# Negated row maxima turned by VectorE in squares of 32 by 32, and sent in four pieces each, in a macaron transformer block

## What is computed

```python
x = x + 0.5 * ffn(layernorm(x))        # weights are signs, hidden width 2048, relu
x = x + attention(layernorm(x))        # 16 heads of 32, w_q, w_k, w_v, w_o
x = x + 0.5 * ffn(layernorm(x))

# attention, per batch and head
scores = einsum('bhqd,bhkd->bhqk', q, k) * SCALE
probs = softmax(scores, axis=-1)
attn = einsum('bhqk,bhkd->bhqd', probs, v)
```

## Time and profile before

| | |
|---|---|
| median of 3 runs | 2874.53 us (2872.97 to 2876.33) |
| the profiled execution | 2881.08 us, span 2879.0 us, mean granted clock of PE 0.997 of full speed |
| PE busy | 2846.1 us, 99% of the span |
| DVE busy | 2041.4 us, 71% |
| ACT busy | 1607.7 us, 56% |
| POOL busy | 1372.8 us, 48% |
| DMA | 424.28 MB in 184375 packets, mean 147 GB/s |
| attention | from about 790 to about 2330 us of the span |

### The profile page before, as it was taken

The page is one execution under the profiler, slowest core; times in us unless marked ns, Lnnn a source line. Parts: engine busy times, 40 slices in busy tenths (PEclk is TensorE's granted clock), DMA queues, the critical chain, the costliest instruction groups (busy, mean ns, idle before and its releaser), DMA issues.

```text
span 2879.0 us, 37964 instructions
## 1 busy us (share of the span) xinstructions
PE 2846.1 (99%) x14288; PEld 1949.0 (68%) x14288; DVE 2041.4 (71%) x3037; ACT 1607.7 (56%) x2850; POOL 1372.8 (48%) x487
## 2 busy tenths in 40 slices
PE   8999999999999999999999999999999999999999
PEld 6888888887755555555555555555555468888887
DVE  5655556768888888888888888888888446555553
ACT  6344434332276767767677777676777654333333
POOL 0000000000089999989898899898988620000000
PEclk9999999999999999999999999999999999999999
DMA  5111112555389999999999999999999962222210
GB/s 190 31 58 30 30 30 71 200 194 188 136 175 194 200 203 202 201 200 203 201 202 204 197 203 202 201 200 200 203 200 204 209 179 59 59 59 59 59 30 30
DMA packets 184375, 424.28 MB, mean 147 GB/s; under 512 B 89728, under 2 KB 90752, under 8 KB 148224
## 3 DMA queue, kind: packets, MB, share of 16 engines
q0 software_dynamic: 31824, 231.75, 39.2%
q1 hardware_dynamic: 152368, 190.11, 24.1%
HBM read 121.91 MB, written 67.63 MB: 66 GB/s over the span
## 4 chain that ended last, share of the span: by engine, by line
PE 84%; DMA 7%; POOL 3%; DVE 3%; issue 2%; ACT 1%; SPq 0%; POOLq 0%; DVEq 0%; ACTq 0%
PE bank L624 16%; PE bank L601 15%; PE bank L1064 15%; PE bank L1060 13%; PE bank L1091 13%; PE bank L743 7%; DMA att_dma_acc<-att_p 3%; PE bank L451 3%; POOL att_acc L924 3%; DMA att_dma_acc<-att_dma_acc 2%; PE bank L1118 1%; DMA prob_sums<-head_total 1%; DMA head_tot_t<-prob_sums 0%; PE bank L240 0%; DMA op_inv_second<-prob_inverse 0%
## 5 line engine op out<-in xcount | busy, mean ns | idle before, releaser
L975 DVE TENSOR_REDUCE att_row_max<-bank 128x1 f32<-128x512 f32 x2048 | 1249.3, 681 | 209.3 <-PE bank L1064 209.1
L924 POOL TENSOR_TENSOR att_acc<-att_acc,att_p 128x2048 f32<-128x2048 f32 x217 | 1079.8, 4976 | 19.7 <-ACT att_p L1044 13.0
L1044 ACT ACTIVATE att_p<-bank 128x512 f32<-128x512 f32 x1792 | 919.4, 617 | 289.3 <-PE bank L1060 286.2
L1064 PE MATMUL bank<-att_k,att_q 96*128 96x512 f32 x2048 | 834.0, 409 | 2.9 <-DVE att_row_max L975 2.6
L1060 PE MATMUL bank<-att_q,att_k 98*128 98x512 f32 x2048 | 810.3, 399 | 6.0 <-ACT att_p L1044 6.0
L1064 PEld LDWEIGHTS bank<-att_k,att_q 96*128 96x128 f32 x2048 | 387.2, 189 | 275.0 <-DVE att_row_max L975 123.2
L1060 PEld LDWEIGHTS bank<-att_q,att_k 98*128 98x128 f32 x2048 | 386.8, 189 | 116.7 <-ACT att_p L1044 17.6
L573 ACT ACTIVATE ffn_hid<-bank,up_s 128x512 f32<-128x512 f32 x256 | 176.3, 689 | 517.2 <-PE bank L601 505.7
L521 DVE TENSOR_TENSOR ffn_hid_lo<-ffn_hid,ffn_hid_hi 128x512 fp32r<-128x512 f32 x256 | 175.7, 691 | 383.7 <-ACT ffn_hid_hi L576 383.7
L1091 PE MATMUL bank<-att_p,att_v 128*32 128x512 f32 x3584 | 434.6, 601 | 0.0
L601 PE MATMUL bank<-hi,ffn_up_w 128*128 128x512 f32 x1024 | 400.7, 391 | 5.7 <-DVE lo L189 3.8
(11 more groups left out here) (116 smaller groups left out, 2378.8 us busy)
## 6 DMA issues: line engine op xcount, KB each, us to landing
att_dma_acc<-att_p POOLq DMA_DIRECT2D x161, 1024.0 KB, 10.6
att_dma_acc<-att_dma_acc POOLq DMA_DIRECT2D x30, 1024.0 KB, 11.9
att_dma_acc<-att_acc POOLq DMA_DIRECT2D x30, 1024.0 KB, 6.9
att_q<-q_hi SPq DMA_DIRECT2D x64, 256.0 KB, 4.1
att_k<-k_hi SPq DMA_DIRECT2D x64, 256.0 KB, 6.7
x<-x_after_ffn SPq DMA_DIRECT2D x15, 1024.0 KB, 7.3
x_after_ffn<-x_out SPq DMA_DIRECT2D x8, 1024.0 KB, 9.9
q_hi<-qkv_o_hi SPq DMA_DIRECT2D x32, 256.0 KB, 2.0
```

What stands on the lines that cost most here:

```text
L924: self.nc.gpsimd.tensor_tensor(self.acc[H % 2][:], a[:], self.tile(H, kt)[:], ALU.add).then_inc(self.summed, 1)
L975: self.nc.vector.tensor_reduce(self.row_max[odd][:, qt, q:q + 1], m[:], axis=AX.X, op=ALU.max).then_inc(self.m_read, 1)
L1044: self.nc.scalar.activation(into[:, q * CH:(q + 1) * CH], self.score_bank(H, kt, q)[:], ACT.Exp, scale=SCALE).then_inc(self.exp_done, 1)
L1064: self.nc.tensor.matmul(m[:], self.q_st[T % NB][0:KQ, qt * P:(qt + 1) * P], self.k_st[T % NB][0:KQ, q * CH:(q + 1) * CH], start=True, stop ...
```

## The change

The negated maxima stay with DVE. neg_max becomes 128 x 32, with columns 16 to 31 zero (set once, in the first head). DVE turns it in four squares of 32 by 32, one for each 32 partitions, into neg_t; so partition 32 i + t of neg_t holds queries 32 i to 32 i + 31 of query tile t. The cast and the subtraction work on 128 x 32 in SBUF. SP sends each of the two rows in four transfers, each from 16 partitions of 32 values, in pieces of 128 bytes. The turn's place in the ring of banks goes (65 places a head), with PE's waits for DVE around it; `rows_out` stands directly behind `negate`. The last head waits for sums_copied before its sums, since these go to bank 3 without a place in the ring that would do it. PE waits for eight transfers a head in place of two.

```diff
--- before.py
+++ after.py
@@ -759,12 +759,14 @@
 UNITS = KT * QC
 AHEAD = LEAD * QC
 GROUP_ENDS, LAST_ENDS = (9, 18, 27, 36, 45, 54, 64), tuple(range(8, 65, 8))
-SUMS_AFTER = TURN_AFTER = 4
-SUMS_AT = TURN_AT = GROUP_ENDS[SUMS_AFTER]
-SLOTS = UNITS + 2
+SUMS_AFTER = 4
+SUMS_AT = GROUP_ENDS[SUMS_AFTER]
+SLOTS = UNITS + 1
 CHAINS = 2
 PER = 7 * 16
-NEG = 3
+NEG = 4
+TURN = 32
+NEG_LOADS = 2 * 16 * (P // TURN)
 ALONE_FROM = 3
 
 
@@ -791,10 +793,10 @@
 
 def slot(p):
 
-    return p + (p >= SUMS_AT) + (p >= TURN_AT)
-
-
-TURN_SLOT, SUMS_SLOT = TURN_AT, SUMS_AT + 1
+    return p + (p >= SUMS_AT)
+
+
+SUMS_SLOT = SUMS_AT
 AT_SLOT = {slot(p): p for p in range(UNITS)}
 
 
@@ -860,13 +862,13 @@
         self.dma_acc = [[c.sb(f"att_dma_acc{i}_{x}", at, [P, SEQ]) for x, at in enumerate(ats)]
                         for i, ats in enumerate(((WORK_AT, SUM_AT), (LO1_AT, X1_AT)))]
         self.row_max = [c.sb(f"att_row_max{i}", HEAD_AT + 4 + 0.25 * i, [P, KT, QC]) for i in range(2)]
-        self.neg_max = c.sb("att_neg_max", HEAD_AT + 4.5, [P, KT])
-        self.neg_hi, self.neg_lo = c.sb("att_neg_hi", HEAD_AT + 5, [KT, P], F32R), c.sb("att_neg_lo", HEAD_AT + 5.5, [KT, P], F32R)
+        self.neg_max, self.neg_t = c.sb("att_neg_max", HEAD_AT + 4.5, [P, TURN]), c.sb("att_neg_t", HEAD_AT + 4.625, [P, TURN])
+        self.neg_hi, self.neg_lo = c.sb("att_neg_hi", HEAD_AT + 5, [P, TURN], F32R), c.sb("att_neg_lo", HEAD_AT + 5.5, [P, TURN], F32R)
         self.m_ps, self.s_ps, self.o_ps = c.bank[0:4], c.bank[4:7], c.bank[7]
         self.loaded = [c.sem(f"att_loaded{i}") for i in range(NB)]
         self.ones_set = c.sem("att_ones_set")
         self.m_ready, self.m_read = c.sem("att_m_ready"), c.sem("att_m_read")
-        self.neg_dve, self.neg_pe, self.neg_loaded = c.sem("att_neg_dve"), c.sem("att_neg_pe"), c.sem("att_neg_loaded")
+        self.neg_set, self.neg_dve, self.neg_loaded = c.sem("att_neg_set"), c.sem("att_neg_dve"), c.sem("att_neg_loaded")
         self.s_ready, self.exp_done, self.p_used = c.sem("att_s_ready"), c.sem("att_exp_done"), c.sem("att_p_used")
         self.summed, self.dma_summed = c.sem("att_summed"), [c.sem(f"att_dma_summed{x}") for x in range(CHAINS)]
         self.chains_joined, self.sum_joined = c.sem("att_chains_joined"), c.sem("att_sum_joined")
@@ -880,9 +882,6 @@
 
 
         return self.m_ps[3] if H >= NH - 2 else self.m_ps[m_bank(H + 1, SUMS_SLOT)]
-
-    def turn_bank(self, H):
-        return self.m_ps[m_bank(H, TURN_SLOT)]
 
 
 
@@ -897,9 +896,10 @@
 
     def max_rows(self, sp, H):
         for r, rows in enumerate((self.neg_hi, self.neg_lo)):
-            sp.wait_ge(self.neg_dve, NEG * H + 2 + r)
-            sp.dma_start(f32(self.q_st[H % NB][KQ + r:KQ + r + 1, :].rearrange("o (t p) -> o t p", p=P)),
-                         f32(rows[:])).then_inc(self.neg_loaded, 16)
+            sp.wait_ge(self.neg_dve, NEG * H + 3 + r)
+            row = self.q_st[H % NB][KQ + r:KQ + r + 1, :].rearrange("o (t i p) -> o i t p", i=P // TURN, p=TURN)
+            for i in range(P // TURN):
+                sp.dma_start(f32(row[:, i, :, :]), f32(rows[i * TURN:i * TURN + KT, :])).then_inc(self.neg_loaded, 16)
 
     def head_free(self, sp, H):
 
@@ -983,16 +983,22 @@
     def negate(self, dve, H):
         dve.wait_ge(self.m_read, UNITS * (H + 1))
         if H > 0:
-            dve.wait_ge(self.neg_pe, H)
-        self.nc.vector.tensor_reduce(self.neg_max[:], self.row_max[H % 2][:], axis=AX.X, op=ALU.max, negate=True).then_inc(self.neg_dve, 1)
-
-    def rows_out(self, dve, H, t_ps):
-        dve.wait_ge(self.neg_pe, H + 1)
+            dve.wait_ge(self.neg_dve, NEG * H)
+        else:
+            self.nc.vector.memset(self.neg_max[:], 0.0).then_inc(self.neg_set, 1)
+            dve.wait_ge(self.neg_set, 1)
+        self.nc.vector.tensor_reduce(self.neg_max[:, 0:KT], self.row_max[H % 2][:], axis=AX.X, op=ALU.max, negate=True).then_inc(self.neg_dve, 1)
+
+    def rows_out(self, dve, H):
+
+        dve.wait_ge(self.neg_dve, NEG * H + 1)
+        self.nc.vector.transpose(self.neg_t[:], self.neg_max[:]).then_inc(self.neg_dve, 1)
+        dve.wait_ge(self.neg_dve, NEG * H + 2)
         if H > 0:
-            dve.wait_ge(self.neg_loaded, 32 * H)
-        self.nc.vector.tensor_copy(self.neg_hi[:], t_ps[0:KT, 0:P]).then_inc(self.neg_dve, 1)
-        dve.wait_ge(self.neg_dve, NEG * H + 2)
-        self.nc.vector.tensor_tensor(self.neg_lo[:], t_ps[0:KT, 0:P], f32(self.neg_hi[:]), ALU.subtract).then_inc(self.neg_dve, 1)
+            dve.wait_ge(self.neg_loaded, NEG_LOADS * H)
+        self.nc.vector.tensor_copy(self.neg_hi[:], self.neg_t[:]).then_inc(self.neg_dve, 1)
+        dve.wait_ge(self.neg_dve, NEG * H + 3)
+        self.nc.vector.tensor_tensor(self.neg_lo[:], self.neg_t[:], f32(self.neg_hi[:]), ALU.subtract).then_inc(self.neg_dve, 1)
 
     def vector_tile(self, dve, H, kt):
         T = H + 1 + (kt + LEAD) // KT
@@ -1002,8 +1008,7 @@
                 self.reduce_block(dve, UNITS * (H + 1) + AHEAD + p, self.m_ps[m_bank(H, slot(p))], T % 2, (kt + LEAD) % KT, q)
             if kt == KT - LEAD and q == 0 and H + 1 < NH:
                 self.negate(dve, H + 1)
-            if p == TURN_AT - 1 and H + 1 < NH:
-                self.rows_out(dve, H + 1, self.turn_bank(H))
+                self.rows_out(dve, H + 1)
         if H > 1 and kt == 2:
             self.head_out.invert(dve, H - 2)
         if H == NH - 1 and kt == 12:
@@ -1074,13 +1079,7 @@
             pe.wait_ge(self.m_read, n - 3)
         elif 2 <= n < FOUR_FROM:
             pe.wait_ge(self.m_read, n - 1)
-        if n == UNITS:
-            pe.wait_ge(self.neg_dve, NEG)
         self.maxima(self.first_bank(n), T, n % UNITS // QC, n % QC)
-
-    def transpose_max(self, pe, H, t_ps):
-        pe.wait_ge(self.neg_dve, NEG * H + 1)
-        self.nc.tensor.transpose(t_ps[0:KT, 0:P], self.neg_max[:], self.ident[:]).then_inc(self.neg_pe, 1)
 
     def out_tile(self, pe, H, kt):
         pe.wait_ge(self.exp_done, UNITS * H + QC * (kt + 1))
@@ -1125,8 +1124,6 @@
             old -= MR
         if old == SUMS_SLOT:
             pe.wait_ge(self.head_out.sums_copied, H)
-        elif old == TURN_SLOT:
-            pe.wait_ge(self.neg_dve, NEG * (H + 2))
         elif old < 0:
             pe.wait_ge(self.m_read, UNITS * (H + 1) + AHEAD + old + 1)
         else:
@@ -1135,7 +1132,7 @@
     def tensor_group(self, pe, H, u, beside=None):
 
         if u == 0:
-            pe.wait_ge(self.neg_loaded, 32 * (H + 1))
+            pe.wait_ge(self.neg_loaded, NEG_LOADS * (H + 1))
             pe.wait_ge(self.ones_set, min(H + 1, NB))
         ends = group_ends(H)
         begin = ends[u - 1] if u > 0 else 0
@@ -1159,11 +1156,10 @@
         if H < NH - 1 or u < ALONE_FROM:
             for kt in range(complete(H, u - 2), complete(H, u - 1)):
                 self.out_tile(pe, H, kt)
-        if u == TURN_AFTER and H + 1 < NH:
-            self.bank_free(pe, H, TURN_SLOT)
-            self.transpose_max(pe, H + 1, self.turn_bank(H))
         if u == sums_after(H) and H > 0:
             self.bank_free(pe, H, SUMS_SLOT)
+            if H == NH - 1:
+                pe.wait_ge(self.head_out.sums_copied, H - 1)
             self.sums(pe, H - 1)
 
 
@@ -1394,8 +1390,7 @@
                             ffn1.add_input(dve, NCH - 1)
                         if (n, t) == (FIRST_TURN[0], FIRST_TURN[1] - 1):
                             att.negate(dve, 0)
-                        if (n, t) == FIRST_TURN:
-                            att.rows_out(dve, 0, att.m_ps[2])
+                            att.rows_out(dve, 0)
 
                 for H in range(NH):
                     for kt in range(KT):
@@ -1505,8 +1500,6 @@
                         qkv.tensor(pe, n, t, between)
                         for b in range(count // 2, count):
                             att.first_maxima(pe, first + b)
-                        if (n, t) == FIRST_TURN:
-                            att.transpose_max(pe, 0, att.m_ps[2])
 
                 pe.wait_ge(qkv.qk_read, 8 * NCH)
                 pe.wait_ge(qkv.v_read, 4 * NCH)
@@ -1519,7 +1512,6 @@
                             first = (H, end, i) == (LAST - 1, UNITS, 0)
                             if first:
                                 pe.wait_ge(att.m_read, UNITS * NH)
-                                pe.wait_ge(att.neg_dve, NEG * NH)
                                 pe.wait_ge(wo_done, DT + 1)
                             if (H, end) == (LAST - 1, UNITS) or (H == LAST and u < 3):
                                 oproj.product(pe, 0, t, range(STEPS * i // count, STEPS * (i + 1) // count))
```

## The result

| | before, same chip | after | ratio, 95% interval |
|---|---|---|---|
| device time, median | 2875.06 us | **2927.28 us** (2924.56 to 2939.18) | 1.0189 [1.0173, 1.0205] |

The change costs 1.9%. The forecast of 2868.5 us and its range up to 2899 both missed. The profiled execution of after took 2939.18 us, span 2937.1, 58.1 more than before's 2879.0. Three rows of its page: the chain by engine, the chain by wait, and the group of the maxima's products with the idle time in front of them and what ended it.

A forecast was written before the change was run, and what follows sets the result against it. PE and the DMA engines had nothing to spare in attention, and PE held 84% of the chain. Terms: -9.9 for the turn + 4 for late rows = -6 us, median about 2868.5 us; range 2862 to 2899.

The forecast's parts named there:

- The turn's price on PE: In attention, removing PE's weight load and matmul saves 0.32 us a head, 31 x 0.32 = 9.9 us, all on the path.
- the prediction's last part: Signs to check in the profile; the distance of two heads, 47.37 us, should be 47.05 if all is hidden.
- DVE's time: Transpose, cast and subtraction in SBUF at 0.24 us each, 0.8 together, free where DVE stood still for 1.32 us.
- The pace of SP's issues: Time per issue of SP's eight row transfers in attention, which decides whether the eighth lands within 14.3 us.
- the middle one: Pace of 0.98 us a piece from eight transfers in a row in attention; the eighth lands at 13.6, 0.7 early.
- The slow row: In attention the low rows hold SP for 1.36 us behind the high ones, and the sums for another 1.36.
- the break-even of 1.15: Pace of SP's issues, 1.15 us, at which PE starts to wait for the rows at a head's start.
- The slow case's arithmetic: At 1.41 us a piece the eighth transfer starts 9.0 us behind the first and lands at 15.8, 1.5 late.
- the sum had 4: Charge for late rows at head starts: a quarter of the heads late by 0.5 us, 4 us.
- Rival 1: Pieces land late, PE's first matmuls of each head wait: 2886 to 2911 us, slower; chance 0.33.
- Rival 3: DMA engines, share 0.97 already, become the bound in attention: +2.5 us, 2877, if PE pays all; chance 0.04.
- The sums' store: SP's store behind the eight transfers: sums back by 1504.1 or 1506.7 us, before DVE's reciprocal at 1506.81.

The follow-up runs named there:

- the runs with more lead: Maxima 28 blocks ahead instead of 20: on after, 3032.04 us in one run, 3090 to 3092 in three; on the version with the bank, 2891.67 us.
- the version with the bank: After, with the squares turned into a PSUM bank that cast and subtraction read, still eight transfers a head: 2900.54 us, ratio 1.0084.
- the two fastest kernels with DVE's turn: Both turn into a PSUM bank, against after: two transfers of constants, 2871.11 us; maxima 28 blocks ahead, negation at a group's end, 2874.57 us.

## Why the prediction was wrong

- **The turn's price on PE: right.** 0.32 us a head; heads with their rows in time are 47.05 us long, as the prediction's last part said. It can be had as 5 us in a median, not 9.9, since half is lost again at the end of attention.
- **DVE's time: right where it ran free, wrong as a rule, and the second step that failed.** 0.18 to 0.21 us for each operation against 0.24, and a first issue 0.5 us behind the negation against 0.6. The sentence "free even at 0.28 each" failed twice. Cast and subtraction took up to 4.4 and 5.3 us, since they wait for POOL. I had priced them by rows whose cast and subtraction read a bank, and the operands' place was what mattered. And it was free by its place alone, as the runs with more lead showed. The term was put at nothing and measured 27 us: 2927.28 with the operands in SBUF, 2900.54 with them in a bank.
- **The pace of SP's issues: the first step that failed, and by a little the larger.** "I take the middle one for the sum": I took 0.98 us a piece from eight larger transfers. The slow row, 1.36 us, was the right one: same tiles, same place, head after head. The pace was 1.41 us, above the break-even of 1.15. I preferred the longer run of issues to the nearer kind. The slow case's arithmetic (eighth issue after 9.0 us, landing after 15.8, 1.5 late) came out: mostly 8 to 10 us, and typically 15.5 in all. With DVE's waits gone, in the version with the bank, the pieces leave 24.3 us over the kernel before; with the 9.9 of the turn that is 34 us, where the sum had 4.
- **Rival 1: right for the pieces, with no place for DVE.** It gave 2886 to 2911, and the version with the bank, where the pieces alone are late, took 2900.54. That after's waits for rows, 41.8 us, are close to its 31 x 1.5 is luck: without DVE's waits they are 23.6. What after adds on top is these later rows, PE's waits for DVE's reductions (10.2 us) and the clock. After a wait of 4.32 us PE in after does this:

```profile
1277.65 0.50 PE L1069 MATMUL bank<-att_k,att_q 96*128 96x512 f32 x1 [4.32 <-DMA att_q<-att_neg_lo]
1277.98 0.40 PE L1065 MATMUL bank<-att_q,att_k 98*128 98x512 f32 x1
1278.22 0.40 PE L1069 MATMUL bank<-att_k,att_q 96*128 96x512 f32 x1
...
1279.06 0.63 PE L1065 MATMUL bank<-att_q,att_k 98*128 98x512 f32 x1
1279.49 0.63 PE L1069 MATMUL bank<-att_k,att_q 96*128 96x512 f32 x1
1279.92 0.63 PE L1065 MATMUL bank<-att_q,att_k 98*128 98x512 f32 x1
```

  Products that started 0.23 us apart start 0.43 apart, at the lower of the two levels. Over the execution the mean clock is 0.990 against 0.997, 0.007 x 2937 = 21 us, an estimate. Less what the profile of before waited in the same places (2.6 us for DVE, and 6.0 for ACT where after waited 0.7), the account is -9.9 + 41.8 + 7.6 - 5.3 + 21 = 55 us, against 58.1 in the spans and 59.9 from the first to the last start of a head.
- **Rival 3, the DMA engines as the bound: wrong.** Their share fell. **The sums' store, "tight at the slow pace"**: nothing waited for it but one reciprocal at the end, 6.9 us, where before waited 8.4.

What POOL does to DVE is stated in the Trainium skill, "SBUF — State Buffer", section "Who interferes with whom": copies and casts in a mode that uses both port pairs contend with POOL, operations with two SBUF inputs contend with its reads, and neither reductions nor operations with at most one SBUF input outside that mode do. The runs agree in what they can show: cast 4.4 us and subtraction 5.3 beside an addition, reduction 0.19 always, and one SBUF input beside the bank 0.19 always. In which mode the cast ran, no run shows. I had not weighed it before the run.

Open: what sets the 1.41 us. It was 0.64 in the projections, and 1.41 under POOL's adding transfers, at 2, 4 and 8 KB alike. The load of the DMA engines is not all of it. In the kernel with the pieces and the turn on PE, the eight for the last head went out like this, at a DMA share of 1.03 from 2290 to 2295 us, the same as the 1.02 beside the eight before them (2242 to 2250):

```profile
2290.51 2.42 SPq L903 DMA_DIRECT2D att_q<-att_neg_hi  x4
2292.97 2.48 SPq L903 DMA_DIRECT2D att_q<-att_neg_lo  x4
```

That is 0.6 us a transfer. No run took the adding transfers away, or issued from another queue. Nor is it shown why the two fastest kernels with DVE's turn run at a mean clock that is lower by 0.001.

## What to carry to other kernels

Take the pace of a queue from the row nearest in kind and place, even if it is two long; in attention the price was by the transfer (1.4 us), whether of 2, 4 or 8 KB. Before an operation moves from PSUM to SBUF on VectorE, look at what GpSimd runs beside it: a 0.2 us cast may last until GpSimd's operation ends, and one here sat out four of them. And work is free only beside the stretch that covers it: when the order changes, ask anew what stands beside each small operation, and add the slower clock after any wait of several microseconds of TensorE.

## What the runs showed of the hardware that was not expected

- A DVE cast of 128 x 32 between SBUF tiles took 0.16 to 0.18 us alone and up to 15.6 us beside POOL's additions. It can miss the gap between two of them: in the row above it began at 876.08 and ended at 885.01, with the second.
- The subtraction at 1311.73 us began 0.37 us ahead of POOL's addition by the profile and yet ended with it. The record of POOL's L935, which issues an adding transfer, was running at that moment (1311.49 to 1312.36). So it was in the two other cases of this kind, at 1465.37 us and at 2116.72 in the kernel with the added cast. Whether that record or a rough start of the addition explains it is open.
- The transpose of 32 by 32 squares between SBUF tiles took 0.21 us in all 32 heads, though POOL was adding at its start in 13.
- Writing the transposed squares to a bank cost 0.23 us against 0.21 in SBUF, and took all waiting for POOL away.
- A wait of 4 us costs PE some 3.4 us more through the clock (an estimate from the granted clock), in the profiled run of after with more lead.
